# Edge sums of a graph network: a small GpSimd fill behind every gather of 128 rows

## The reference

```
ft = (feat @ W).reshape(n, H, D)
a1 = einsum('nhd,hd->nh', ft, attn_l)
a2 = einsum('nhd,hd->nh', ft, attn_r)
e = leaky_relu(a1[src] + a2[dst], 0.2)
ex = exp(e - segment_max(e, dst)[dst])
alpha = ex / segment_sum(ex, dst)[dst]
out = segment_sum(ft[src] * alpha, dst)
```

## Time and profile before

| | us |
|---|---|
| timed runs, median of 3 | 1890.75 |
| profiled execution, span from first to last instruction | 2276.6 |
| `edge_sums`, one head, in the profiled execution | 676.1 |
| `edge_sums`, eight heads, in the profiled execution | 757.0 |
| POOL busy with the 784 gathers | 745.7 |
| POOL idle ahead of gathers | 719.3 |

### The profile page before, as it was taken

One profiled execution on the slowest core, in us unless ns is written; L12 is line 12 of the kernel. 1 busy time (PEld: TensorE's weight loads), 2 busy tenths in 40 slices (PEclk: granted clock), 3 DMA queues, 4 the chain that ended last, 5 costly groups with the idle time before them and its releaser, 6 DMA issues. The chain is left out here.

```text
span 2276.6 us, 34460 instructions
## 1 busy us (share of the span) xinstructions
PE 1646.4 (72%) x9468; PEld 1342.0 (59%) x9468; DVE 1163.6 (51%) x3309; ACT 656.1 (29%) x2160; POOL 1009.6 (44%) x1093
## 2 busy tenths in 40 slices
PE   5177776677778978999463665777577777689991
PEld 4045555556656557999343554555455556689991
DVE  7256566555456664222452555556566657841223
ACT  4222121122322554333152222332222212643330
POOL 4556555656543002555124545555454541325550
PEclk9588888889889989999786777888787989599996
DMA  7323222333222016666532222222222220267666
GB/s 167 98 71 84 80 75 75 87 82 87 78 70 58 1 63 224 211 213 210 135 112 72 80 74 77 74 80 75 70 77 68 72 72 20 93 199 213 215 202 178
DMA packets 148002, 244.24 MB, mean 107 GB/s; under 512 B 53369, under 2 KB 83368, under 8 KB 147558
## 3 DMA queue, kind: packets, MB, share of 16 engines
q0 software_dynamic: 48384, 134.19, 21.1%
q1 hardware_dynamic: 97306, 106.27, 15.7%
q10 hardware_dynamic: 2124, 1.54, 0.3%
HBM read 210.48 MB, written 31.21 MB: 106 GB/s over the span
## 5 line engine op out<-in xcount | busy, mean ns | idle before, releaser
L679 POOL DMA_INDIRECT es_rows<-table,eall x784 | 745.7, 951 | 719.3 <-SPq L668 418.6
L699 PE MATMUL bank<-es_msg,es_one 128*125 128x264 f32 x976 | 305.3, 466 | 123.5 <-DVE es_msg L822 104.1
L699 PE MATMUL bank<-es_rows,es_won 128*125 x976 | 289.8, 448 | 116.8 <-DVE es_won L819 84.8
L762 ACT ACTIVATE es_oneT<-bank 125x512 bf16<-125x512 f32 x244 | 145.1, 595 | 755.9 <-remote 488.5
L699 PEld LDWEIGHTS bank<-es_msg,es_one 128*125 128x125 f32 x976 | 209.0, 225 | 175.2 <-DVE es_msg L822 113.9
L699 PEld LDWEIGHTS bank<-es_rows,es_won 128*125 128x125 f32 x976 | 202.4, 218 | 159.2 <-issue 125.3
L842 DVE TENSOR_TENSOR es_z<-es_rows,es_near 128x4 f32<-128x4 f32 (+1 forms) x244 | 43.1, 177 | 359.3 <-ACTq L774 265.2
L1237 PE MATMUL bank<-ffn_xbT,ffn_w 128*128 128x128 f32 x1792 | 220.8, 277 | 0.0
L1290 ACT ACTIVATE xT<-bank,ffn_b1s 128x128 f32<-128x128 f32 x448 | 128.2, 369 | 303.2 <-PE bank L1237 292.6
L1396 DVE TENSOR_TENSOR xT<-bank,xT 128x256 f32<-128x256 f32 x112 | 47.6, 425 | 327.8 <-issue 190.1
L1247 PE MATMUL bank<-ffn_w,xT 128*128 x896 | 211.7, 379 | 0.0
(11 more groups left out here) (445 smaller groups left out, 2408.8 us busy)
## 6 DMA issues: line engine op xcount, KB each, us to landing
ffn_w<-in_L_ffn_W SPq DMA_DIRECT2D x112, 512.0 KB
es_rows<-table,eall POOLq DMA_INDIRECT x784
ffn_w<-yrows SPq DMA_DIRECT2D x20, 560.0 KB
ffn_w<-in_L_ffn_W SPq DMA_DIRECT2D x2, 4096.0 KB
xrows<-acc SPq DMA_DIRECT2D x10, 560.0 KB
table<-acc SPq DMA_DIRECT2D x5, 577.5 KB
table<-acc SPq DMA_DIRECT2D x5, 564.4 KB
out_x<-xs SPq DMA_DIRECT2D x5, 560.0 KB
```

Source lines behind the costliest of these rows:

```text
L679: pool.indirect_dma_start(rows[:, q % R, w, :], None, m.table[H], bass.IndirectOffsetOnAxis(ap=m.eall[:, at:at + 1], axis=0)).then_inc(gat ...
L699: ins = pe.matmul(sum_banks[p % 2][0:P, 0:W], left, right, start=(w == 0), stop=(w == BW - 1))
L762: a.activation(oneT[:, p % 2, :], turn_bank[0:P, :], ACT.Copy).then_inc(kept, 1)
```

## The change

A scratch row of 96 bytes in each of 128 partitions is allocated, and a semaphore `spaced`. Behind every gather POOL fills that row with zeros. From the second fill on, each waits until the fill before it is done. Nothing reads the row.

```diff
+        apart = sb("_apart", [128, 96], mybir.dt.uint8)
...
-        ends_set, laid, ready = sem("_ends_set"), sem("_laid"), sem("_ready")
+        ends_set, laid, ready, spaced = sem("_ends_set"), sem("_laid"), sem("_ready"), sem("_spaced")
...
                         pool.indirect_dma_start(rows[:, q % R, w, :], None, m.table[H],
                                                 bass.IndirectOffsetOnAxis(ap=m.eall[:, at:at + 1], axis=0)).then_inc(gathered[q % R], 16)
+                        if at > 0:
+                            pool.wait_ge(spaced, at // 2)
+                        pool.memset(apart[:, :], 0).then_inc(spaced, 1)
```

## The result

The kernel became slower by about 20 us: 1910.85 us (median of 4 runs, 1907.22 to 1916.46) against 1890.51 (4 runs, 1889.61 to 1891.35), a ratio of 1.0109 with a 95% interval of 1.0089 to 1.0128. The forecast had the sign right and the size far too large: +92 us.

A forecast was written before the change was run, and what follows sets the result against it. The prediction took POOL's gathers, issued 1.25 us apart, to bound the edge stages: 1890.75 us plus 110 for 784 fills of 0.14, less 18 of room, gives 1983 us, range 1886 to 2070.

The forecast's parts named there:

- the price of a fill, 0.14 us: On POOL, each fill behind a gather adds 0.14 us, the pitch among fills; 784 of them make 110 us.
- the room, 18 us: In the timed edge stages, 18 us remain beside the gathers' pitch and the stage ends, and absorb that much added need.
- The excess of the disturbed execution: The 385.85 us by which the profiled span exceeds timed runs are delays inside the two edge stages.
- The price of a gather: On POOL, a gather costs its start-to-start pitch of 1.253 us, gap of 0.30 included; 784 take 982 us.
- Rival A: Gathers don't bound the timed runs, or the fill hides in POOL's 0.30 us gap: 1890 us, chance 0.16.
- The lower bound of 0 and the upper of 0.48: Limits for one fill on POOL: 0 if it fits the gap, 0.48 us for its duration plus another gap.
- the cores which write descriptors: On POOL, a pair of cores writes DMA descriptors and does its fill share between gathers, so the fill counts in full.
- 2 x 23.6 us: Time from the last gather's start to the stage's end, 23.6 us in the first edge stage, assumed alike in both.
- The waits cost nothing: On POOL, the 782 added waits cost nothing, since the earlier fill is long done and one gather covers the hand-over.
- Rival B: Fills space the gathers, letting other engines' updates through, so the kernel gets faster: 1858 us, chance 0.09.
- Rival C: Each fill costs POOL up to 0.48 us with a gap of its own: up to 2249 us, chance 0.12.
- A span that grows by far less than the timed runs do: In the profile after, the 110 us would mostly lie inside POOL's 418.6 us of waiting, so its span grows much less.

The follow-up runs named there:

- experiment 3: Against the changed kernel, each fill writes 1 byte a partition instead of 96, semaphore and waits kept: 1890.94 us, ratio 1.0005 to the kernel before.
- experiment 5: Against the changed kernel, each fill writes 48 bytes a partition instead of 96: 1897.73 us, ratio 1.0028 to the kernel before.
- experiment 1: The kernel before, unchanged, profiled once more: 1888.8 us.
- experiment 11: Against the kernel before, no fills, the eight-head stage's mixer makes keys two tiles a step, so its later parts stand 12 steps earlier: 1883.28 us, ratio 0.9956.

## Why the prediction was right in sign and wrong in size

That the gathers' pitch on POOL sets the time and that a fill lengthens it was right. Two terms of the sum were mis-sized: the price of a fill, 0.14 us, and the room, 18 us. The price is the step that failed most: with it alone put right the sum gives +34 us, with the room alone put right some +80; measured are +20.

- **The excess of the disturbed execution lies in the edge stages, and timed runs have next to no waiting for slots: right.** 24.4 us of such waits are left in the undisturbed execution, and its stages are 153 and 232 us shorter than the 676.1 and 757.0 of the earlier trace rows.
- **The price of a gather is its pitch, 1.25 us, and not its duration of 0.95: right.** The Trainium skill's advice in "Perfetto Trace Analysis", "GPSIMD Engine Instruction", to time this engine from start to start agrees: by starts the fill costs 0.06 us, by durations it would cost 0.195.
- **"I take 0.14" for a fill: the term that failed.** It measured 0.06 where nothing holds the gathers up and 0.067 in the mean. 784 x 0.067 = 52 us of more need, not 110. The prediction read the gap of 0.30 as a part of the gather's price, and beside it charged the pitch of fills among fills in full. But of the fill's 0.195 us, 0.13 lies in that gap. Experiments 3 and 5 show it: 0.12 us is free, and by the rule of experiment 5 what is beyond 0.30 - 0.165 = 0.135 counts. Rival A, "the fill hides in the gap", held for two thirds of each fill. The lower bound of 0 and the upper of 0.48 held the value; I chose by the row that looked most like it and gave too little weight to the lower one.
- **That the cores which write descriptors do their share of the fill between two gathers, so that it counts in full: not borne out.** A third of it counts. The prediction worked this out from two statements of the Trainium skill, in "GPSIMD Engine Reference", "4. When to use GPSIMD" and "2.1 Instruction dispatch"; the page itself gives no price for a fill behind a gather. What POOL does in the gap no run shows.
- **"18 us" of room: too small.** Of the 52 us of need 20.3 were paid, so some 30 went into room; two fills give 36. The 18 counted POOL's pauses alone, and as that it was about right: they were 20.5 us (experiment 1). What follows the last gather it took as fixed, 2 x 23.6 us that come later with the gathers (its own rows give 33.9 for the second stage: 1933 - 1899.1). But the last score didn't wait for its rows: it came 9.3 and 26.5 us behind the last gather, where 2.0 is enough. This lead is room too. The pauses gave 16 us (4.3 are left), the leads 7.1 and 6.5; with the 20.3 paid that makes 50 us, near the 52. The prediction also counted one sum over both stages, while the gathers bind by stretches: in the eight-head stage up to block 53, where each 0.067 counts (14.4 us), not at all behind it; in the one-head stage only once some 20 us of room are used up (392 x 0.067 = 26, 6.6 paid).
- **The waits cost nothing, and a queue that is one gather ahead is enough: right** within 0.17% (experiment 3, which has both).
- **Rival B, faster by spacing: not seen.** No kernel with fills is clearly faster than the same one without. The delays of 19 us on which it rested belong to the disturbed execution; the waits for a nameless sender are gone from the other.
- **Rival C, a gap of its own for each fill: not for one fill.** Nor for the second of two: it has no cover left and counts in full, 0.22 us, but brings no further gap of 0.30.
- **"A span that grows by far less than the timed runs do": could not be seen.** The profiled execution of after was undisturbed, 1910.2 us.

## What to carry to other kernels

Before an added instruction is priced, look at the gap that it lands in: here a gap put down to "issue" took in 0.12 us of work, and only what stuck out was paid. Then ask in which stretch the lengthened queue is the last to arrive; the distance from a transfer's end to its first use, step by step, gives that, and where it is at its floor the price is paid in full; elsewhere it comes out of the lead and is free until that is used up. The same map tells where to put other work: what was moved out of the stretch that the other engines set, into one that waits for gathers, was a gain of 8 us (experiment 11).

## What was not expected of the hardware

- A gather of 128 rows by GpSimd keeps 0.30 us of gap to the next one when nothing stands between, but the gap behind a fill between them is only 0.165 (0.19 behind a fill of 0.12 us).
- A fill of bytes takes about as long per element as one of four-byte numbers: 121 ns for one byte a partition, 156 for 48 and 195 for 96, so 0.78 ns a byte, against 0.83 an element in the earlier trace rows.
- A profiled execution was 20% longer than all timed runs of the same kernel (2276.6 us against 1890.51), with the excess in waits of two stages and a granted clock there of 0.84 and 0.81 instead of 0.92 and 0.94. What disturbed it stays open; no run was made on that.
